# Attention on one core: order of VectorE's small operations, layout of the score banks in PSUM

## The reference

```python
q = (h @ w_qc @ w_qup).reshape(b, t, H, D).transpose(0, 2, 1, 3)      # H = 8, D = 64
q = _rmsnorm(_apply_partial_rope(q, cos, sin), g_qnorm)
k = _rmsnorm(_apply_partial_rope(h @ w_k, cos, sin), g_knorm)
v = h @ w_v
kc, vc = (z.reshape(b, nb, 32, D).mean(2) for z in (k, v))            # two blocks of 32 keys
pc = softmax(concat([where(safe, q @ kc * scale, NEG), sink]))        # over blocks
ps = softmax(where(tok_sel, q @ k * scale, NEG))                      # over keys
pw = softmax(concat([where(sw, q @ k * scale, NEG), sink]))           # over keys, with the sink
g = sigmoid(q @ w_gate + b_gate); g = g / clip(g.sum(-1), 1e-06)
mixed = g[..., 0:1] * comp_out + g[..., 1:2] * sel_out + g[..., 2:3] * sw_out
y = einsum('btgf,gfi->btgi', group(mixed), w_out_group).reshape(b, t, 128) @ w_out
x1 = _layernorm(h + y)
```

## Time and profile before

| | us |
|---|---|
| median of three runs | 769.38 (768.86 to 769.88) |
| the profiled execution | 767.93 |
| its span in the trace | 766.1 |
| mean granted clock of TensorE | 0.89 |

### The profile page before, as it was taken

The page is one execution under the profiler, slowest core; times in us unless marked ns, Lnnn a source line. Parts: engine busy times, 40 slices in busy tenths (PEclk is TensorE's granted clock), DMA queues, the critical chain, the costliest instruction groups (busy, mean ns, idle before and its releaser), DMA issues.

```text
span 766.1 us, 17009 instructions
## 1 busy us (share of the span) xinstructions
PE 566.3 (74%) x4773; PEld 430.0 (56%) x4773; DVE 554.0 (72%) x1891; ACT 444.2 (58%) x1363; POOL 460.7 (60%) x553
## 2 busy tenths in 40 slices
PE   4766777777777775797998897873109898989864
PEld 2444555555555554465676665552008888888831
DVE  2589999999999985368688988963406666666514
ACT  2588777878787772496687565430005555555515
POOL 4568777777777753555556487778741444445533
PEclk9999889999998897598999999885559999999998
DMA  6144444531111111200111111011111222122164
GB/s 233 55 161 174 172 149 145 179 122 34 34 44 33 37 31 31 73 26 22 36 40 40 36 54 33 29 50 46 53 45 50 66 58 71 53 70 61 37 204 130
DMA packets 69468, 57.78 MB, mean 75 GB/s; under 512 B 22133, under 2 KB 64250, under 8 KB 67074
## 3 DMA queue, kind: packets, MB, share of 16 engines
q1 hardware_dynamic: 64450, 46.14, 19.5%
q0 software_dynamic: 4352, 8.47, 3.3%
q10 hardware_dynamic: 576, 2.10, 0.7%
HBM read 25.86 MB, written 31.33 MB: 75 GB/s over the span
## 4 chain that ended last, share of the span: by engine, by line
PE 19%; issue 17%; POOL 15%; DMA 3%; DVE 3%; ACT 2%; SPq 1%; POOLq 0%; ACTq 0%; DVEq 0%
PE ps L1300 8%; POOL l_keys L957 6%; POOL disp_dram L982 5%; PE ps L1325 4%; PE ps L1306 2%; PE ps L1336 2%; POOL l_rs L964 2%; POOL x_xr L969 2%; DMA l_R<-y_dram 1%; PE ps L1280 1%; DMA out_x<-l_keys 1%; ACT l_keys L1398 1%; POOL y_dram L1409 1%; POOL l_W1l L973 1%; PE ps L827 1%
## 5 line engine op out<-in xcount | busy, mean ns | idle before, releaser
L1409 POOL DMA_INDIRECT y_dram<-l_keys,m_blk x72 | 70.5, 979 | 97.2 <-ACT l_keys L1376 83.2
L350 ACT ACTIVATE a_E<-a_ps,a_nb,a_sc 128x64 f32<-128x64 f32 x256 | 99.6, 408 | 10.6 <-DVE a_nb L473 9.6
L431 POOL TENSOR_TENSOR a_rinv<-a_ms,a_halfneg 128x9 f32<-128x9 f32 x32 | 57.7, 1803 | 33.4 <-DVE a_ms L546 33.4
L309 PE MATMUL a_ps<-a_tab,a_xTt 128*128 128x512 f32 x64 | 38.9, 692 | 46.9 <-DVE a_r L488 41.5
L982 POOL DMA_INDIRECT disp_dram<-l_R,x_pos x64 | 62.9, 983 | 17.5 <-issue 17.3
L957 POOL TENSOR_TENSOR l_keys<-x_kT,l_table 128x1024 f32<-128x1024 f32 x32 | 62.0, 1937 | 6.7 <-ACT x_kT L906 6.4
L1441 DVE TENSOR_SCALAR m_lin<-ps 128x512 f32<-128x512 f32 x36 | 24.9, 691 | 49.5 <-PE ps L1306 48.4
L964 POOL TENSOR_TENSOR l_rs<-x_ve,l_halfneg 128x2 f32<-128x2 f32 x32 | 23.9, 748 | 57.2 <-DVE x_ve L1113 56.9
L350 ACT ACTIVATION_READ_ACCUMULATOR a_E<-a_ps,a_nb,a_sc 128x1 f32 x256 | 53.3, 208 | 0.0
L1376 ACT ACTIVATE l_keys<-ps,m_blk 128x128 f32<-128x128 f32 x72 | 22.6, 364 | 44.1 <-PE ps L1325 43.5
L1022 DVE TENSOR_SCALAR l_R<-x_r,x_mv,l_rs 128x256 f32<-128x256 f32 x32 | 20.3, 635 | 35.1 <-POOL l_rs L964 27.7
(11 more groups left out here) (234 smaller groups left out, 1943.8 us busy)
## 6 DMA issues: line engine op xcount, KB each, us to landing
disp_dram<-l_R SPq DMA_DIRECT2D x16, 1040.0 KB, 4.2
m_blk<-disp_dram SPq DMA_DIRECT2D x72, 65.0 KB
a_xTt<-in_xT SPq DMA_DIRECT2D x32, 64.0 KB, 3.8
...
a_VB<-v_dram SPq DMA_DIRECT2D x128, 16.0 KB, 2.0
...
```

The source lines that it names most:

```text
L309: nc.tensor.matmul(flat[:, 0:512], xTt[:, a.u2, :], wqkv[:, 0:512], start=True, stop=True)
L350: last = nc.scalar.activation(E[:, e.u4, g, :], ps_Sh[:, g // 4, g % 4, 0:D], ACT.Exp, bias=nb[:, e.u2, g:g + 1], scale=sc8[:, e.u4, g:g + 1],
L431: G.tensor_tensor(rinv[:, b.u4, :], ms[:, b.u2, :], halfneg[:, 0:9], ALU.pow).then_inc(inv_rms, 1)
L1409: G_.indirect_dma_start(out=Y[:, :], out_offset=bass.IndirectOffsetOnAxis(ap=blk[:, (2 * q + j) % NB, P:P + 1].bitcast(I32), axis=0), in_= ...
```

## The change

All of it lies in `attention`.

- PSUM: the scores use a ring of banks 4, 5 and 6, two per tile (for t mod 3 = 1 in reverse order); a bank waits for the exponentials that last read it, counted by halves of a tile. Turned probabilities move to bank 7, and mixed values share bank 2 with the turned queries.
- TensorE: scores are made bank by bank; `y` of k stands before the transposes of d; the mixed values of h wait for `qT_copied` of d.
- ScalarE: `exped` is raised per half tile; the sums go straight into `den`.
- GpSimd: both sine halves in one instruction; both powers move ahead of the mixing, and the variance of k is the tenth column of the mean squares of b while tile b exists; the factor 1/8 goes into the norm weights `gg`, and L433 is gone.
- VectorE: the maximum comes first, then the residual of k, the sum of squares, the statistics, the means of the keys, the variance, the layer norm of l, block scores, rope, arguments, weights. The sink is a third column of the block scores (`u3`), so that one reduction and one subtraction take the place of two each. The weights are formed as reciprocals of den x gate denominator x sum. 35 instructions per slot become 28 (29 for t mod 3 = 1).

```diff
-        ps_S = ps[:, 4:6, 0:GW]
-        ps_Sh = ps_S.rearrange("p a (h w) -> p a h w", w=W)
-        ps_PT, ps_mT = ps[:, 6, :], ps[:, 7, :]
+        ps_PT, ps_mT = ps[:, 7, :], ps[:, 2, :]
+
+        def ps_S(t):
+
+            halves = (ps[:, 4:6, 0:GW], ps[:, 6:3:-2, 0:GW], ps[:, 5:7, 0:GW])[t % 3]
+            return halves, halves.rearrange("p a (h w) -> p a h w", w=W)
...
+
+        def rstd(t):
+
+            if t + 7 < tiles:
+                return rinv[:, (t + 7) % 4, 9:10], inv_rms, t + 8
+            return rs[:, t % 2:t % 2 + 1], ln_rstd, t + 8 - tiles
...
                 if e.live:
                     e.wait(pe, qT_copied)
                     e.wait(pe, k_means)
-                    e.free(pe, exped, 1)
+                    S, _ = ps_S(e.t)
                     for j in range(2):
-                        nc.tensor.matmul(ps_S[:, j, :], idb[:, :], maskb[:, :], start=True, stop=False,
+                        if 2 * e.t + j >= 3:
+                            pe.wait_ge(exped, 2 * e.t + j - 2)
+                        nc.tensor.matmul(S[:, j, :], idb[:, :], maskb[:, :], start=True, stop=False,
                                          skip_group_check=True)
+                        for c in range(2):
+                            for q in range(2):
+                                last = nc.tensor.matmul(
+                                    S[D * q:D * q + D, j, c * 2 * W:(c + 1) * 2 * W],
+                                    qT[:, e.u2, 2 * j + c, D * q:D * q + D],
+                                    KB[:, e.u2, q, :, :].rearrange("p h w -> p (h w)"),
+                                    start=False, stop=True, skip_group_check=True)
+                    last.then_inc(scored, 1)
+                if k.live:
+                    k.wait(pe, mT_copied)
+                    k.free(pe, y_added, 1)
+                    before = Tile(at, 1)
+                    if before.live:
+                        before.wait(pe, squared)
                     for c in range(4):
-                        for q in range(2):
-                            last = nc.tensor.matmul(
-                                ps_S[D * q:D * q + D, c // 2, (c % 2) * 2 * W:(c % 2 + 1) * 2 * W],
-                                qT[:, e.u2, c, D * q:D * q + D],
-                                KB[:, e.u2, q, :, :].rearrange("p h w -> p (h w)"),
-                                start=False, stop=True, skip_group_check=True)
-                    last.then_inc(scored, 1)
+                        last = nc.tensor.matmul(ps_y, mT[:, c, :], wc[:, c, :], start=(c == 0), stop=(c == 3))
+                    last.then_inc(y_done, 1)
                 if d.live:
                     d.wait(pe, roped)
                     d.wait(pe, k_normed)
@@ -292,15 +308,6 @@
                                             qk[:, d.u4, 2 * c:2 * c + 2, :].rearrange("p h d -> p (h d)"), idf[:, :])
                     nc.tensor.transpose(ps_kT, kd[:, d.u2, :, :].rearrange("p h d -> p (h d)"),
                                         idf[:, :]).then_inc(turned, 1)
-                if k.live:
-                    k.wait(pe, mT_copied)
-                    k.free(pe, y_added, 1)
-                    before = Tile(at, 1)
-                    if before.live:
-                        before.wait(pe, squared)
-                    for c in range(4):
-                        last = nc.tensor.matmul(ps_y, mT[:, c, :], wc[:, c, :], start=(c == 0), stop=(c == 3))
-                    last.then_inc(y_done, 1)
...
                     h.wait(pe, PT_copied)
                     h.wait_ring(pe, v_spread, 64)
                     h.free(pe, mT_copied, 1)
+                    if d.live:
+                        d.wait(pe, qT_copied)
...
                 if e.live:
                     e.wait(act, maxed)
                     e.free(act, mixed, 4)
-                    for g in range(H):
-                        last = nc.scalar.activation(E[:, e.u4, g, :], ps_Sh[:, g // 4, g % 4, 0:D], ACT.Exp,
-                                                    bias=nb[:, e.u2, g:g + 1], scale=sc8[:, e.u4, g:g + 1],
-                                                    accum_out=Z[:, e.u2, g:g + 1])
-                    last.then_inc(exped, 1)
+                    e.free(act, mixing, 2)
+                    _, Sh = ps_S(e.t)
+                    for j in range(2):
+                        for g in range(4 * j, 4 * j + 4):
+                            last = nc.scalar.activation(E[:, e.u4, g, :], Sh[:, j, g % 4, 0:D], ACT.Exp,
+                                                        bias=nb[:, e.u2, g:g + 1], scale=rinv[:, e.u4, g:g + 1],
+                                                        accum_out=den[:, e.u2, g, 1:2])
+                        last.then_inc(exped, 1)
...
-                    G.tensor_tensor(tb[:, :, 0:16], q[:, :, 16:32],
-                                    sin[:, 0:16].unsqueeze(1).to_broadcast([P, 9, 16]), ALU.mult)
-                    G.tensor_tensor(tb[:, :, 16:32], q[:, :, 0:16],
-                                    sin[:, 16:32].unsqueeze(1).to_broadcast([P, 9, 16]),
+                    G.tensor_tensor(tb[:, :, :].rearrange("p h (w k) -> p h w k", w=2),
+                                    q[:, :, 0:32].rearrange("p h (w k) -> p h w k", w=2)[:, :, ::-1, :],
+                                    sin[:, :].rearrange("p (w k) -> p w k", w=2).unsqueeze(1).to_broadcast([P, 9, 2, 16]),
                                     ALU.mult).then_inc(sined, 1)
...
+                if k.live:
+                    k.wait(pool, ln_var)
+                if k.live and not b.live:
+                    G.tensor_tensor(rs[:, k.u2:k.u2 + 1], ve[:, :], halfneg[:, 0:1], ALU.pow).then_inc(ln_rstd, 1)
+                if b.live:
+                    b.wait(pool, mean_sq)
+                    b.free(pool, exped, 4, 2)
+                    b.free(pool, x1_done, 11)
+                    w = 10 if k.live else 9
+                    G.tensor_tensor(rinv[:, b.u4, 0:w], ms[:, b.u2, 0:w], halfneg[:, 0:w],
+                                    ALU.pow).then_inc(inv_rms, 1)
                 if f.live:
                     f.wait(pool, mixing)
                     f.free(pool, P_turned, 2)
@@ -422,15 +443,6 @@
                     G.tensor_tensor(
                         Pv, Pv, pc[:, f.u2, :, :].rearrange("p h n -> p (h n)").unsqueeze(2)
                         .to_broadcast([P, 2 * H, 32]), ALU.add).then_inc(mixed, 1)
-                if k.live:
-                    k.wait(pool, ln_var)
-                    G.tensor_tensor(rs[:, k.u2, :], ve[:, k.u2, :], halfneg[:, 0:1], ALU.pow).then_inc(ln_rstd, 1)
-                if b.live:
-                    b.wait(pool, mean_sq)
-                    b.free(pool, exped, 4)
-                    G.tensor_tensor(rinv[:, b.u4, :], ms[:, b.u2, :], halfneg[:, 0:9], ALU.pow).then_inc(inv_rms, 1)
-                    b.wait(pool, inv_rms)
-                    G.tensor_tensor(sc8[:, b.u4, :], rinv[:, b.u4, 0:H], root[:, :], ALU.mult).then_inc(scales, 1)
...
         def slot(at):
                 b, c, d, e, f, k, l = (Tile(at, m) for m in (1, 2, 3, 4, 5, 8, 9))
+                if e.live:
+                    e.wait(dve, scored)
+                    _, Sh = ps_S(e.t)
+                    parts = (slice(0, 1), slice(1, 2)) if e.t % 3 == 1 else (slice(0, 2),)
+                    mx2, s52 = (v.rearrange("p (a h) w -> p a h w", a=2) for v in (mx[:, :].unsqueeze(2), s5[:, e.u2, :, :]))
+                    for part in parts:
+                        n_max = n.add(V.tensor_reduce(mx2[:, part, :, 0], Sh[:, part, :, 0:D], AX.X, ALU.max))
+                    e.free(dve, gate_args, 2)
+                    for part in parts:
+                        last = V.tensor_copy(s52[:, part, :, :], Sh[:, part, :, D:W])
+                    last.then_inc(scores_kept, 1)
+                    n.upto(n_max)
+                    e.wait(dve, inv_rms)
+                    e.free(dve, exped, 2, 2)
+                    V.scalar_tensor_tensor(nb[:, e.u2, :], mx[:, :], -1.0, rinv[:, e.u4, 0:H], ALU.mult,
+                                           ALU.mult).then_inc(maxed, 1)
+                if k.live:
+                    k.wait(dve, y_done)
+                    k.wait_ring(dve, x_in, 16)
+                    k.free(dve, x1_done, 2)
+                    V.tensor_tensor(r[:, k.u2, :], ps_y, xt[:, k.u2, :], ALU.add).then_inc(y_added, 1)
+                if b.live:
+                    b.wait(dve, squared)
+                    n_ss = n.add(V.tensor_reduce(ss[:, :], sq[:, b.u2, :, :], AX.X, ALU.add))
+                if k.live:
+                    k.wait(dve, y_added)
+                    n_bn = n.add(V.bn_stats(st[:, :], r[:, k.u2, :]))
+                if b.live:
+                    n.upto(n_ss)
+                    b.free(dve, inv_rms, 2)
+                    V.tensor_scalar(ms[:, b.u2, 0:9], ss[:, :], 1.0 / D, 1e-6, ALU.mult, ALU.add).then_inc(mean_sq, 1)
+                if k.live:
+                    n.upto(n_bn)
```

(49 more changed lines are left out.)

117 lines of the change are left out of this document (15 added, 102 removed).

## The result

The changed kernel takes 868.58 us (median of four runs, 865.27 to 871.05) against 769.63 for the kernel before: 1.128 times as long, 95% interval 1.124 to 1.132. The forecast of 826 had the sign and the mechanism; the time lies above its range of 800 to 850. The profiled execution took 865.27 us, its span is 863.5, 97.4 more than before.

What follows compares the result with a forecast made beforehand. VectorE was taken to bound the kernel before, a 9.73 us loop the changed one; with 0.9 for the clock, 10.6 a slot. 24 slots +50.0, tail +11, head -4: +57, so 826 us, range 800 to 850.

Steps and rivals of the forecast that it cites:

- What bounds the kernel before: Attention stage: VectorE's order sets the 8.515 us slot, with 1.7 us of standing beside GpSimd's mixing.
- The loop, 9.73 us: Each steady slot: mixing, transposes, scores, y, variance, power, mixing close a loop of 9.73 us against 8.515.
- The clock in the loop, +0.9 a slot: TensorE's low clock now lies on the loop and adds 0.9, making 10.6 us a slot.
- The upper bound: Loop with the whole of it at the low clock: 11.69 us a slot, 854 us in all.
- about half of one low stretch: One low-clock stretch of TensorE in every slot, about half of it on the loop: 0.9 us.
- Tail, +11, and head, -4: From slot 32 to the last residual add: 11 us more; slots 4 to 7, without the variance loop: 4 less.
- SyncE's loads cost nothing: SyncE's queue keeps its order and its loads come a slot or more ahead: no cost.
- Ring, shared bank, TensorE's new wait: nothing: Score banks cost nothing in steady slots; TensorE's wait for copied queries is covered, at most 0.49 us uncovered.
- (b): Rival: no difference, the loop being 8.5 us by chance, 769 us; chance 0.03.
- (a): Rival: loop shorter than its rows' sum, ScalarE's round decides, 8.0 us a slot with small waits, 751 us; chance 0.10.
- (c): Rival: GpSimd's power keeps VectorE's two-input instructions out, 11.0 us a slot, 836 us; chance 0.04.
- The signs named ahead: Slot near 10.6 us, GpSimd idle 1.5 to 2, TensorE idle about 3, VectorE's share about 60 to 80%.

Runs made afterwards that it cites:

- warm: The changed kernel plus 26 matmuls into columns nobody reads, filling TensorE's standing before the mixing arrives; 798.24 us, 1.049 of the kernel before.
- split_power: The changed kernel with the two powers taken apart again, mean squares still ahead of the mixing, variance behind it; 803.35 us, 1.059 of the kernel before.
- psum_only: The kernel before with only the change's PSUM and TensorE part, VectorE's and GpSimd's instructions and order as before; 758.63 us, 0.999 of the kernel before.
- mix_mid: The changed kernel with GpSimd's two mixing passes done before the variance wait and the ten-element power; 744.03 us, 0.979 of the kernel before.
- no_power_warm: The changed kernel with the ten-element power replaced by a subtraction and 14 matmuls added in TensorE's standing; 762.43 us, 1.002 of the kernel before.
- mix_mid_turns: The changed kernel with the mixing ahead of the powers and TensorE's query and key transposes back ahead of y; 725.82 us, 0.957 of the kernel before.

## Why the prediction was right or wrong

- **What bounds the kernel before:** right. VectorE was the bound, with standing for GpSimd in it. Its busy time per slot fell from 8.36 to 6.87 us (51.85 / 90 x 11.93); that its share is 58% comes from the longer slot as well. With the loop open the change brings 2.1%, and 5.8% with the mixing first and TensorE's transposes put back.
- **The loop, 9.73 us:** right, link by link. With the clock held up the slot is 9.72 to 9.74. The ten-element power took 1.994, forecast 1.95. The largest error of a link was y's, 1.00 (156.53 to 157.53 in `warm`) for 0.89; small errors the other way cancel it.
- **The clock in the loop, +0.9 a slot:** this step failed. Measured are 11.93 - 9.73 = 2.2. The 24 slots thus cost 82.05 where 50.0 were put, 32 us of the 42.6 by which the forecast missed the median; tail and head add 8 and 3, the rest behind them takes off 2.7, and about 2 are the distance of the profiled execution from the median. The step has two faults. The upper bound was summed wrongly: it stretched the transposes, the scores and the turned queries to the low level, but not y, which had moved into the loop; at the low level y to the transposes behind it takes 188.50 - 186.63 = 1.87 instead of the 0.89 of the earlier trace rows. All low is therefore 9.73 + 1.41 + 0.98 + 0.55 = 12.67 and not 11.69, and the upper end of the whole 24 us higher, 878 instead of 854, which is above the result. Even so it is not a bound in each step: transposes and scores took 3.86 in one turn where the earlier trace rows have 3.55. And "about half of one low stretch" was a choice with no row behind it: the granted clock is 0.77 in the stage, hence low for 46% of the time, and the low part falls on the matmuls right behind the standing, which is where the loop runs (0.53 and 0.68 there, 1.00 outside). The old trace had both kinds of low stretch: in the stage, where the longest standing was 2.2 us, every second slot took 2.44 to 2.60 from the transposes to behind the scores, and the one of the earlier trace rows, behind 3.81 us of standing, took 3.55. The loop's standing was forecast at 3.1 and measured at 3.7 to 3.9, so the second kind was the one to expect. The rule of the Trainium skill that was set beside it, "TensorE: Matmul & The Clock Gate", section "What's actually happening", that the throttled state is the default and activity releases it, pointed to the upper end; the runs agree in that: 11.93 without the added matmuls and 9.75 with them.
- **Tail, +11, and head, -4:** +19.1 and -1.1. In the tail the last three full slots took 12.3, 11.2 and 9.7 where 10.6, 8.4 and 8.4 had been put; `warm`, with the clock held up, has 9.7, 8.6 and 8.6 there, so this is the low clock again. The three short ones took 6.76 instead of 5.9, at a granted clock of 0.74. In the head, slots 6 and 7 took 9.95 and 9.54, for two reasons. At the end of slot 7 TensorE waited 3.3 us for the mixing, which stands behind the power of the mean squares as soon as there is something to mix; the loop was reckoned from slot 8 on, with the variance, and split_power shows that the shorter one exists by itself. In slot 6 TensorE waited 3.9 us for a load of the next rows (first row below). It had been issued at 35.54, behind a fill of 1040 KB issued at 34.91, and the faster slots 4 and 5 (4.4 and 6.0 us) had come up to it; that the fill delayed it is likely and not isolated by a run. That SyncE's loads cost nothing was wrong there, once.

The waits from 28 to 58 us of the changed kernel (who for whom, total us, times, longest):

```profile
PE a_ps L316 <- DMA a_xTt<-in_xT: 3.9, 1, 3.9
...
PE a_ps L271 <- POOL a_Pm L443: 3.3, 1, 3.3
```

- **Ring, shared bank, TensorE's new wait: nothing.** Right as far as the runs go: psum_only is 0.999, with VectorE as the bound.
- **Rivals:** (b) did not come. (a) did not come either, and its price was sound: 7.9 to 8.0 a slot was worked out for ScalarE's own round, and mix_mid, where the loop is open, has 7.88 in most slots. (c), the power keeping VectorE's two-input instructions out, did not come: in the changed kernel the cosine (L532) took 0.44 inside the power of 191.27 to 193.27, and the slot of `warm` is the sum without that term. The rule behind it, "SBUF — State Buffer" of the Trainium skill, section "SBUF: two separate sides", holds here for the mixing passes, in both directions (L570 of the change takes 0.81 beside the mixing, 0.18 in mix_mid without it; the mixing takes 1.34 behind the cosine in no_power_warm), and not for the power.
- **The signs named ahead** came in kind and larger than told, as the slot did: 11.93 us instead of 10.6; VectorE's share 58%, just under 60 to 80%; GpSimd idle before the power 2.0 to 3.1 us instead of 1.5 to 2, TensorE before the transposes 3.7 to 3.9 instead of 3.

What stays open: why the slots of `mix_mid_turns` change between 7.09 and 7.63, mostly in threes. A wait of GpSimd's gates for the block scores (1.6 us at most) stands highest in its list, and it is gone with the mixing moved; no run isolates it.
